# The two maximum tiles of a slot behind its fourth score product, the values ahead of its third, in a decoder layer on one core

## The reference

```python
x = _layernorm(x + attn(x))       # three rounds of attention, 16 heads of 16
x = _layernorm(x + xattn(x, ctx_1024, mask))
x = _layernorm(x + ffn(x))        # base product plus the best of 8 adapters, chosen by a reconstruction loss

# xattn, per batch: 16 heads of 16
scores = jnp.einsum('bhqd,bhkd->bhqk', q, k) / jnp.sqrt(jnp.float32(D_HEAD))
attn = jax.nn.softmax(jnp.where(mem_mask, scores, -jnp.inf), axis=-1)
out = jnp.einsum('bhqk,bhkd->bhqd', attn, v)
```

## Time and profile before

| what | value |
|---|---|
| median of 3 runs | 1941.04 us (1934.62 to 1941.15) |
| the profiled execution | 1936.46 us, of it 1934.6 us span |
| TensorE products busy | 1696.2 us, 88% |
| VectorE busy | 1254.5 us, 65% |
| ScalarE busy | 1068.0 us, 55% |
| GpSimd busy | 186.6 us, 10% |
| mean granted TensorE clock | 0.948 of full speed |
| chain that ended last | PE 67%, ACT 12%, issue 4%, DVE 3%; by line: values L823 20%, scores L806 17%, exponentials L918 11%, pair tiles L783 10% |

### The profile page before, as it was taken

The page is one execution under the profiler, slowest core; times in us unless marked ns, Lnnn a source line. Parts: engine busy times, 40 slices in busy tenths (PEclk is TensorE's granted clock), DMA queues, the critical chain, the costliest instruction groups (busy, mean ns, idle before and its releaser), DMA issues.

```text
span 1934.6 us, 25301 instructions
## 1 busy us (share of the span) xinstructions
PE 1696.2 (88%) x9566; PEld 636.7 (33%) x9566; DVE 1254.5 (65%) x1802; ACT 1068.0 (55%) x2079; POOL 186.6 (10%) x146
## 2 busy tenths in 40 slices
PE   5654588899999999999999999999999999999966
PEld 3443122233323332333333333333233333332223
DVE  3332877677667767777677767776777667776412
ACT  2320066666666665566566656666656655665650
POOL 5611010010001000010001100100001000000000
PEclk7765599999999999999999999999999999999997
DMA  2421060524052505152223405250515132320000
GB/s 100 79 46 45 29 127 24 99 69 81 19 84 89 92 20 84 61 89 46 47 55 104 79 14 84 89 92 22 84 59 104 34 60 39 75 31 1 5 21 14
DMA packets 99578, 115.93 MB, mean 60 GB/s; under 512 B 20729, under 2 KB 84986, under 8 KB 99458
## 3 DMA queue, kind: packets, MB, share of 16 engines
q1 hardware_dynamic: 96722, 113.27, 29.1%
q10 hardware_dynamic: 2736, 1.06, 0.2%
HBM read 79.51 MB, written 34.77 MB: 59 GB/s over the span
## 4 chain that ended last, share of the span: by engine, by line
PE 67%; ACT 12%; issue 4%; DVE 3%; ACTq 1%; POOLq 0%; POOL 0%; DVEq 0%
PE values L823 20%; PE banks L806 17%; ACT xprobs L918 11%; PE banks L783 10%; PE work L710 4%; PE work L698 3%; PE work L667 3%; PE work L720 2%; PE work L715 2%; PE work L703 1%; PE work L722 1%; DVE xneg_max_pieces L1107 1%; PE work L659 1%; PE work L730 1%; PE work L670 1%
## 5 line engine op out<-in xcount | busy, mean ns | idle before, releaser
L918 ACT ACTIVATE xprobs<-banks 128x512 f32<-128x512 f32 x1664 | 902.6, 596 | 529.4 <-PE banks L806 507.3
L1107 DVE TENSOR_REDUCE xneg_max_pieces<-banks 128x2 f32<-128x1024 f32 x768 | 913.6, 1219 | 222.8 <-PE banks L783 217.2
L806 PE MATMUL banks<-xq_stacks,xk_stacks 99*128 99x512 bf16 (+1 forms) x1664 | 541.6, 386 | 87.9 <-ACT xprobs L918 60.0
L823 PE MATMUL values<-xprobs,xv_rows 128*17 128x512 f32 x3328 | 437.9, 598 | 1.0 <-ACT xprobs L918 1.0
L806 PEld LDWEIGHTS banks<-xq_stacks,xk_stacks 99*128 99x128 bf16 (+1 forms) x1664 | 128.3, 97 | 649.8 <-ACT xprobs L918 554.1
L783 PE MATMUL banks<-xk_stacks,xq_stacks 49*128 49x512 bf16 (+1 forms) x2048 | 257.6, 341 | 28.7 <-DVE xneg_max_pieces L1107 18.8
L1177 POOL TENSOR_TENSOR xk_parts<-xk_rest,xk_parts 128x401 bf16<-128x401 f32 (+1 forms) x64 | 59.9, 938 | 849.7 <-ACT xk_parts L883 849.4
L783 PEld LDWEIGHTS banks<-xk_stacks,xq_stacks 49*128 49x128 bf16 x2048 | 58.1, 95 | 183.9 <-issue 121.0
L823 PEld LDWEIGHTS values<-xprobs,xv_rows 128*17 128x17 f32 x3328 | 55.1, 95 | 154.8 <-ACT xprobs L918 90.9
L1042 DVE TENSOR_TENSOR xk_rest<-work,xk_parts 128x401 f32<-128x401 f32 (+1 forms) x64 | 36.8, 576 | 70.6 <-PE work L698 47.9
L1069 DVE SCALAR_TENSOR_TENSOR err<-work,wdec_bdec,hT 128x512 f32<-128x512 f32 x30 | 22.5, 750 | 79.1 <-PE work L722 79.1
(11 more groups left out here) (218 smaller groups left out, 1223.6 us busy)
## 6 DMA issues: line engine op xcount, KB each, us to landing
xk_stacks<-key_parts_dram SPq DMA_DIRECT2D x192, 200.1 KB, 12.2
key_parts_dram<-xk_parts SPq DMA_DIRECT2D x144, 100.0 KB, 1.8
xq_stacks<-parts_dram SPq DMA_DIRECT2D x192, 64.0 KB, 8.0
ctxT_a<-in_ctxT SPq DMA_DIRECT2D x4, 1601.0 KB, 8.0
ctxT_b<-in_ctxT SPq DMA_DIRECT2D x4, 1601.0 KB, 8.4
parts_dram<-xq_parts SPq DMA_DIRECT2D x48, 128.0 KB, 1.7
key_parts_dram<-xk_parts SPq DMA_DIRECT2D x48, 100.2 KB, 9.2
xa<-in_x SPq DMA_DIRECT2D x8, 512.0 KB, 3.8
```

Of the source, the lines that this page charges most:

```text
L806: pe.matmul(scores[n % SRING], kst[0:ROWS[par], k, h2, par, t * P:(t + 1) * P], qst[0:ROWS[par], k, h2, par, :], start=True, stop=True).th ...
L823: last = pe.matmul(av[32 * j:32 * j + HD + 1, :], vals[:, k, t, gr * GH + j, :], probs[:, sl % 2, j, :], start=t == 0, stop=t == XKT - 1)
L918: nc.scalar.activation(probs[:, sl % 2, j, :], scores[n % SRING], ACT.Exp).then_inc(exped, 1)
L1107: nc.vector.tensor_reduce(nmp[:, of % 2, j2, :, q, piece], pairs[n % MRING][:, :, :], AX.X, ALU.max, negate=True).then_inc(mxr, 1)
```

## The change

`pe_slot` issues the two pair tiles of a slot behind the fourth score, and with that the values of the slot before stand directly behind the second score (or the first of two jobs).

```diff
             pe_scores(m, t, 1)
             if len(jobs) > 1:
                 pe_job(MAIN, jobs[0])
-            for one in todo:
-                pe_next_pair(*one)
             if m or t:
                 pe_values(XKT * m + t - 1)
             pe_scores(m, t, 2)
             pe_scores(m, t, 3)
+            for one in todo:
+                pe_next_pair(*one)
             if jobs:
                 pe_job(MAIN, jobs[-1])
```

## The result

The changed kernel takes 2011.08 us in the median of 4 runs (2008.32 to 2021.03), against 1940.9 for the kernel before (1934.62 to 1941.15). The ratio over all these runs is 1.0375, with a 95% interval of 1.0341 to 1.041: it is 3.75% slower (the two medians alone are 3.6% apart). The forecast had the sign (1965 us, 1.2% slower) but a third of the size, and its range ended at 1988.

A forecast was written before the change was run, and what follows sets the result against it. TensorE was taken to set the pace, also standing for exponentials. Terms -52 -12 +11 +16 +30 +20 +14 gave +27 us on 1936.46, so 1963.5; forecast median 1965 us, 1.2% slower, range for 8 in 10 1940 to 1988.

The forecast's parts named there:

- Slots without a job: 92 slots where the moved tiles fill the hole behind the fourth score: 3.41 to 2.87 us each, -52 us in all.
- The wait for the maxima (`max`): Slot 9: the maxima's transposition waits for L1131, behind the first tile's maximum on VectorE; slot 4.28 instead of 3.13, +30 us.
- `mid`: Stage 2, slot 8: the job waits for adapter weights because VectorE's choice ends later; start 4.8 instead of 2.8, +14 us.
- Two-job slots, +20 us: Stage 0, slots 2, 8 and 10: `oT`, `x1T`, `x2T` wait for VectorE work behind the maxima; +20 us over seven batches.
- Slots with a long job, 0.09 more in the hand-over, +11 us: Some 136 slots without holes: one more change between product kinds on TensorE, 0.09 each, taken as +11 us.
- Slots behind a short job or such a slot, -12 us: Some 8 slots in each of seven batches: the 0.27 hole before the second score is filled, 0.20 shorter each, -12 us.
- Exponential late, +16 us: Slots behind encoder jobs and slot 12 of stages 0 and 2: late exponentials no longer covered by tiles, +16 us.
- second rival: Gain and loss cancel: `mid` in time (-14), hand-over free (-11); 1938.5, or 1943 with the median's 4.6; chance 0.16.
- VectorE keeps up: Rival: holes are filled and the waits behind VectorE don't come, leaving -37 us, 1900; chance 0.10.
- VectorE's delay feeds on itself: Rival: late VectorE holds the next slot's job bank and third exponential, +55 us more, about 2020; chance 0.10.

The follow-up runs named there:

- max_first: Changed kernel with VectorE's three steps on the finished maxima of slot 9 put ahead of that slot's first tile maximum; 1983.29 us, ratio 1.0225 to the kernel before.
- tiles_between: Changed kernel with the pair tiles between third and fourth score in slots with a longer job; 2000.19 us, ratio 1.0319 to the kernel before.
- best: Changed kernel plus early tiles before `oT`/`x1T`, slot 9 maxima steps first, choice finished in slot 5, long-job tiles after third score, maxima copy before second tile's maximum; 1904.44 us.
- before_vector: Kernel before the change with only two VectorE queue edits: finished-maxima steps first in slot 9, adapter choice finished in slot 5; 1939.25 us, ratio 0.9998.

## Why the forecast was wrong in size

- **Slots without a job**: right, 0.54 each, 2.87 us, -49.3 against -52. The measured period at the end of the main block was a good stand-in.
- **The wait for the maxima (`max`)**: right in place and size, 4.14 against 4.12 us into the slot, +29.5 against +30, shown by `max_first`. The same for the starts of `oT` (2.43 against 2.39) and `mid`, whose first product starts 4.73 us into slot 8 of stage 2 (1017.16 to 1021.89) against 4.8:

```profile
1016.70 0.13 DVE L1026 CAST adp<-sc 1x1 int32<-1x1 f32 x1
...
1021.89 3.57 PE L730 MATMUL work<-x2T,wdown 128*64 128x512 f32 x4 [1.90 <-DMA bdown_col<-in_bdown]
```

- **"Two-job slots, +20 us"** is the term most off: +40.2. The starts were right, what came behind them ran at half clock: 16 of the 25 drops lie in these slots, some 25 us. The step that failed is that the forecast's sum had no term for the clock at all. It took every duration from rows at the upper level, since the main block before had no other behind its first 20 us, and it put in seven waits of 2 us for each of two jobs and thirty of 1.5 without asking what the clock does after them. 25 drops by 1.58 are 39 us of the profiled execution. The median of the runs is 10 us below it, at mean granted clocks of 0.933 to 0.937 against 0.931; whether they had fewer drops isn't recorded.
- **"Slots with a long job, 0.09 more in the hand-over, +11 us"** was half the size: +0.19 to +0.20 a slot, +30.4 on 135 slots (some of it drops). The hand-over was there as taken (0.54). That the job's first product would take 0.1 longer behind the tiles was not in the sum; no row before had a tile and then a job. `tiles_between` shows it, for `kproj`.
- **"Slots behind a short job or such a slot, -12 us"** gave -5.7. The hole of 0.27 was filled behind a short job, but with 0.19 for the hand-over and the first product a slot gains 0.08 and not 0.20. Behind a slot without a job it was not filled: slot 5 of stage 3 has its second score at 0.49 before and after, and got 0.20 longer.
- **"Exponential late, +16 us"** gave +19.7, near enough.
- With the 39 us of the clock and 15 us for the first products (135 slots by 0.11), both estimates, the forecast's 27 becomes 81, against 83.4 measured.
- **From the sum to the median** the forecast slipped too: 1963.5 and the 4.6 us that it names are 1968, not 1965; its second rival does add them.
- **The rivals**: that VectorE keeps up didn't happen. That VectorE's delay feeds on itself didn't either: the slots behind late VectorE work start their jobs at the usual 2.59, and waits for the tile banks stay small (TensorE's products before L783, 0.5 us). That this rival's 2020 lies near the measured time is chance. The large loss came by a way that none of them named.

Why the clock fell at some of the waits and not at others (slot 10 of stage 1 had a drop in two of eight batches) the runs don't say.

## What to carry to other kernels

A tile moved into another engine's hole is also moved in time for the engine that reads it. So look for every instruction queued behind that read on the reading engine, and for who waits for it: here the filled holes gave 50 us, and the waits behind VectorE, with the drops that followed them, took 87. Repair those waits, and place the tiles by the job of the slot, and the same move pays (1904 us). Making the move only in the slots where it gains isn't the way out: a slot with early tiles behind one with late tiles asks for four tiles at once. And where a change puts waits of 1.5 to 2 us into a TensorE that runs nearly without holes, add what the clock may do afterwards: here 1.6 us for each drop, as much as the wait itself, behind about half of the waits.

## What the hardware showed unexpectedly

- At waits of TensorE of 1.5 to 2.1 us, put into a block that had run at 2.4 GHz for 1600 us, its clock went to 1.2 GHz for 3.4 us, 25 times; the same slot took 4.67 us instead of 3.09. With most of the waits gone, 3 and then 0 such stretches were left. Seven waits of 1.56 us had none in two profiles (the kernel before, `best`) and two in a third (`before_vector`).
- A float32 job of four products (`kproj`) lasted 1.45 us directly behind the 49-row pair tiles and 1.35 behind a full score product; by the trace its second product starts 0.44 us behind the first instead of 0.34, and its first weight load starts with the first product instead of 0.21 ahead.
- VectorE's maxima of two tiles of 1024 columns take 2.36 us, and of four in a row 4.62: 1.18 and 1.16 each, whether the tiles come early or late in the slot.
